# The second half of six matches moved from VectorE to ScalarE in a recommendation tower's opening

## What is computed

```
e = stack([tbl_k[ids[:, k]] for k in range(26)], axis=1)
combined = concatenate([dense[:, None, :], e], axis=1)
interactions = einsum('bnd,bmd->bnm', combined, combined)[:, TRIU_I, TRIU_J]
h = concatenate([dense, interactions, dense], axis=1)
h = maximum(h @ W_top1 + b_top1, 0)
h = maximum(h @ W_top2 + b_top2, 0)
y = h @ W_top3
```

## Time and profile before

| | before |
|---|---|
| median of 3 runs | 385.69 us |
| the profiled execution | 386.84 us |
| its span | 384.9 us |
| TensorE matmul busy | 343.2 us (89%) |
| VectorE busy | 193.3 us (50%) |
| ScalarE busy | 125.5 us (33%) |
| GpSimd busy | 251.9 us (65%) |
| mean granted TensorE clock | 0.986 |
| chain that ended last | PE 69%, POOL 17%, issue 8%, DVE 3% |

### The profile page before, as it was taken

How to read it: one execution, slowest core, us unless ns; L and a number is a source line. 1 busy time by engine, 2 the same in 40 slices (tenths; PEclk the granted TensorE clock), 3 DMA queues, 4 the chain that set the end, 5 groups by cost and what they waited for, 6 DMA issues and landing times.

```text
span 384.9 us, 13108 instructions
## 1 busy us (share of the span) xinstructions
PE 343.2 (89%) x6048; PEld 304.9 (79%) x6048; DVE 193.3 (50%) x94; ACT 125.5 (33%) x211; POOL 251.9 (65%) x267
## 2 busy tenths in 40 slices
PE   0787877889999999999999999999999999965995
PEld 0787767788888988889888988989888988854763
DVE  2799997577424872269243962288334942000000
ACT  2344432343233423343223423343223423322122
POOL 5777887777777777777777777777777777100200
PEclk9999999999999999999999999999999999968999
DMA  8996698253624362264525362256325332321300
GB/s 166 251 219 179 171 296 252 58 192 94 188 57 161 108 203 56 56 200 120 154 58 192 82 198 58 80 181 163 101 56 192 85 86 58 135 55 53 126 11 0
DMA packets 30869, 49.57 MB, mean 129 GB/s; under 512 B 17500, under 2 KB 17636, under 8 KB 30687
## 3 DMA queue, kind: packets, MB, share of 16 engines
q1 hardware_dynamic: 22494, 31.82, 27.7%
q0 software_dynamic: 8320, 16.92, 17.0%
HBM read 38.21 MB, written 10.49 MB: 127 GB/s over the span
## 4 chain that ended last, share of the span: by engine, by line
PE 69%; POOL 17%; issue 8%; DVE 3%; DMA 1%; ACT 1%; DVEq 0%
PE look_ps L309 26%; POOL rows L290 17%; PE mid_ps L339 12%; PE layer_ps L356 11%; PE layer_ps L365 7%; PE mid_ps L321 7%; PE layer_ps L353 4%; DVE match L450 3%; PE layer_ps L372 2%; DMA rows<-in_table,index 1%; DMA index<-in_index 1%; ACT hidden L515 0%; ACT hidden L521 0%; ACT turned L495 0%; ACT y_row L528 0%
## 5 line engine op out<-in xcount | busy, mean ns | idle before, releaser
L290 POOL DMA_INDIRECT rows<-in_table,index x256 | 248.7, 971 | 79.3 <-issue 77.7
L450 DVE TENSOR_TENSOR match<-look_ids,row_number_ps 125x2048 fp32r<-125x2048 int32 x80 | 181.8, 2287 | 126.0 <-PE look_ps L309 119.4
L309 PE MATMUL look_ps<-match,table_high 125*128 125x256 f32 x640 | 164.1, 294 | 21.3 <-DVE table_low L458 19.1
L309 PE MATMUL look_ps<-match,table_low 125*128 125x256 f32 x640 | 157.8, 284 | 0.3 <-issue 0.3
L309 PEld LDWEIGHTS look_ps<-match,table_high 125*128 125x128 f32 x640 | 123.3, 193 | 26.8 <-issue 16.8
L309 PEld LDWEIGHTS look_ps<-match,table_low 125*128 125x128 f32 x640 | 123.6, 193 | 0.0
L339 PEld LDWEIGHTS mid_ps<-turned 128*32 128x32 f32 x4096 | 45.6, 110 | 26.6 <-issue 22.7
L339 PE MATMUL mid_ps<-turned 128*32 128x27 f32 x4096 | 54.8, 196 | 12.5 <-issue 7.4
L488 ACT COPY turned<-look_ps 128x512 f32<-128x512 f32 x40 | 31.8, 799 | 68.3 <-PE look_ps L309 68.3
L495 ACT COPY turned<-mid_ps 128x512 f32<-128x512 f32 x64 | 42.9, 671 | 21.9 <-PE mid_ps L321 17.7
L356 PE MATMUL layer_ps<-pairs,w_pairs_sb 117*128 117x256 f32 x192 | 48.0, 386 | 0.0
(11 more groups left out here) (21 smaller groups left out, 44.8 us busy)
## 6 DMA issues: line engine op xcount, KB each, us to landing
look_ids<-in_look_rows SPq DMA_DIRECT2D x40, 256.0 KB
scratch<-grams SPq DMA_DIRECT2D x8, 864.0 KB
rows<-in_table,index POOLq DMA_INDIRECT x256
scratch<-grams SPq DMA_DIRECT2D x8, 416.0 KB
pairs<-scratch SPq DMA_DIRECT2D x92, 29.2 KB
grams<-in_table SPq DMA_DIRECT2D x4, 448.0 KB
pairs<-in_table SPq DMA_DIRECT2D x3, 448.0 KB
hidden<-in_table SPq DMA_DIRECT2D x3, 448.0 KB
```

The costliest lines, as they stand in the source:

```text
L290: pool.indirect_dma_start(out=rows[j % 2][:, at, :], out_offset=None, in_=tables[GATHERED[at]], in_offset=bass.IndirectOffsetOnAxis(ap=ind ...
L309: last = nc.tensor.matmul(look_ps[pair % 2][:, r % 2, :], part[0:table_rows, r, c, :], match[number % 2][0:table_rows, c, :], start=(c == ...
L450: nc.vector.tensor_tensor(match[number % 2][0:table_rows], look_ids[b][0:table_rows, r % 2].unsqueeze(1).broadcast_to(shape), row_number_p ...
```

## The change

For the first six looks of group 1, VectorE compares only parts 0 to 3. ScalarE makes parts 4 to 7 with two kinds of instruction: |id + (−row)| by Abs with the negated row number as a per-partition bias, one instruction for each of the four parts (256 elements), then Relu(1 − x) over all four (1024 elements), which is 1 where the id is the row and 0 elsewhere. Look (1, r) waits for both. VectorE makes the negated row numbers once. SyncE's loads of look ids into slots that these halves read wait for the halves too. On ScalarE the first half stands between split_high(0) and split_high(1), and the half for r = 1 to 5 at the head of the loop's round r, ahead of take_look and take_turned.

```diff
+        minus_row = sbuf("minus_row", [P, PARTS])
...
                 if number >= ID_SLOTS:
                     sp.wait_ge(match_ready, pair_end(number - ID_SLOTS))
+                    if ID_SLOTS <= number < ID_SLOTS + AHEAD:
+                        sp.wait_ge(second_halves, (number - ID_SLOTS + 1) // 2 * 2)
...
                 pe.wait_ge(match_ready, number + 1)
+                if g == 1 and r < AHEAD:
+                    pe.wait_ge(second_halves, r + 1)
...
-                shape = [table_rows, PARTS, N]
+
+                parts = PARTS // 2 if g == 1 and r < AHEAD else PARTS
+                shape = [table_rows, parts, N]
                 nc.vector.tensor_tensor(
-                    match[number % 2][0:table_rows],
+                    match[number % 2][0:table_rows, 0:parts],
                     look_ids[b][0:table_rows, r % 2].unsqueeze(1).broadcast_to(shape),
-                    row_number_ps[0:table_rows].unsqueeze(2).broadcast_to(shape),
+                    row_number_ps[0:table_rows, 0:parts].unsqueeze(2).broadcast_to(shape),
                     ALU.is_equal).then_inc(match_ready, 1)
...
+            nc.vector.tensor_scalar(minus_row[:], row_number[:], -1.0, None, ALU.mult).then_inc(row_numbers_copied, 1)
...
+            def match_second_half(r):
+
+                number, pair = look_number(1, r), pair_number(1, r // 2)
+                b = pair % ID_SLOTS
+                act.wait_ge(look_ids_in[b], 16 * (pair // ID_SLOTS + 1))
+                after(act, look_done, number - 1)
+                half = match[number % 2][0:table_rows, PARTS // 2:PARTS]
+                for c in range(PARTS // 2):
+                    last = nc.scalar.activation(half[:, c], look_ids[b][0:table_rows, r % 2], ACT.Abs,
+                                                bias=minus_row[0:table_rows, PARTS // 2 + c:PARTS // 2 + c + 1])
+                last.then_inc(distances_made, 1)
+                act.wait_ge(distances_made, r + 1)
+                flat = half.rearrange("p c n -> p (c n)")
+                nc.scalar.activation(flat, flat.bitcast(fp32), ACT.Relu, bias=1.0, scale=-1.0).then_inc(second_halves, 1)
...
-            for r in range(RAWS):
-                split_high(r)
+            split_high(0)
+            act.wait_ge(row_numbers_copied, 2)
+            match_second_half(0)
+            split_high(1)
+            split_high(2)
             for r in range(AHEAD):
+                if r > 0:
+                    match_second_half(r)
                 if r % 2 == 1:
                     take_look(0, r // 2)
                     take_look(1, r // 2)
```

More of the change, by code:

```diff
@@ L116, in build @@
         match_ready = sem("match_ready")
+        distances_made = sem("distances_made")
+        second_halves = sem("second_halves")
         look_done = sem("look_done")
@@ L463, in _ @@
             nc.vector.tensor_copy(row_number_ps[:], row_number[:]).then_inc(row_numbers_copied, 1)
+            nc.vector.tensor_scalar(minus_row[:], row_number[:], -1.0, None, ALU.mult).then_inc(row_numbers_copied, 1)
             for b in range(2):
                 nc.vector.memset(turned[b][:, N * FEATURES:], 0.0).then_inc(pads_zeroed, 1)
-            dve.wait_ge(row_numbers_copied, 1)
+            dve.wait_ge(row_numbers_copied, 2)
             for r in range(LOOKS):
```

## The result

The changed kernel took **396.59 us** (median of 4 runs, 393.57 to 398.02), the kernel before 385.76 in the same comparison (384.72 to 387.26): a ratio of 1.024, 95% interval 1.017 to 1.030. The forecast was 396.6 in a range of 391.7 to 402.5. Medians here are over all runs, while ratios leave out each run that lies over 1.5% above the fastest of its kernel, so the two can differ by some tenths of a percent.

The account below looks back on a forecast made before the run. Bound taken: GpSimd's gathers up to 88.48 us, then TensorE, with VectorE full in the opening. 386.84 + 9.0 − 1.8 + 3.7 = 397.7, less 1.15 for the median: 396.6 us, range 391.7 to 402.5.

Parts of the forecast that it names:

- ScalarE's order is the loss: Opening: each half waits behind the previous turn's copy and a cast, each look for its half; gram(0, 0) 9.0 us later.
- The total, 396.6: Whole kernel: forecast median 396.6 us, from 397.7 for the profiled execution less 1.15; chance of this case 0.50.
- the rival's sum: Opening: TensorE's clock cold in every round or halves nearer 3.1 us; 402.1 us, 1.8 more if both; chance 0.20.
- VectorE, 6.8 us less: Opening: six matches cut from 2048 to 1024 elements, about 1.1 us saved each, 6.8 us in all off VectorE.
- The half, 2.75 us: ScalarE's added work per look: four Abs 1.61, Relu 1.04, two hand-overs of 0.05; 2.75 us, between 2.5 and 3.1.
- Look(1, 1) at 26.06: Opening: its half waits for raw table 3 and a cast, so this look starts at 26.06 us instead of 20.93.
- Rounds of 6.89 and 7.10, look(1, 5) at 54.04: Opening loop: even rounds 6.89 us, odd 7.10, where a round was 5.7; the last of these looks starts at 54.04.
- The clock, 3.7 us: Opening: idle gaps drop TensorE's clock in the first round and one later one, 1.8 + 1.9 = 3.7 us more.
- Gather waits, −1.8: TensorE's two waits for gathered rows, 0.97 and 0.83 us, the second at turn(1, 7), vanish: 1.8 us back.
- In the opening VectorE is the full engine: Opening: VectorE's round is two matches, 4.70 us, and a split, 1.22; splits stand 5.7 us apart.
- The rival that was faster: Opening: splits miss GpSimd's gathers, so turn(1, 7) and the end come 3.1 us sooner, 382.6 us; chance 0.04.
- One that comes out early would stand at turn(1, 7): End of the gathers: a TensorE early out of the opening would still wait there for rows; the turn started at 91.10.

Follow-up runs that it names:

- the quarter: Against the changed kernel, ScalarE makes only parts 6 and 7 and VectorE six parts: 384.97 us, ratio 0.990; run once more 386.57 us, 1.001.

## Why the prediction was right

- *ScalarE's order is the loss*: right. With the same work in another place the ratio is 1.002 and not 1.015, and the waits for the halves are gone. Filler matmuls bring the ratio to 1.002 as well with the order as it is, so a large part of the loss is the cold clock behind the gaps that the order makes; the sum had both. The length of a step follows ScalarE's piece: with half of the match 7.0 and 7.2 us without a cold clock, with a quarter 5.8 and 6.0, 1.2 less for a piece that is 1.2 shorter.
- *The total, 396.6*: 396.59, and the closeness is luck. The sum made the profiled execution 397.7 and it took 396.51; taking off 1.15 for the median then hit, since the profile of the changed kernel lay at its own median. By its terms TensorE should have been 10.9 us late once the gathers' waits were used up, and it was 9.06; the growth behind that, which the sum did not have, made up for a part. On the second chip the loss was 5.7 us and not 10.8. The upper bound of 402.5 is not the rival's sum either, which is 402.1, or 403.9 with the slower halves.
- *VectorE, 6.8 us less*: 5.8. A match of 1024 elements took 1.22 us and not half of 2.28, so the matches are 6.4 us shorter in all.
- *The half, 2.75 us*: 2.93 from the first Abs to the look. The Abs took 1.71 for 1.61, the Relu 1.06 for 1.04, the wait on ScalarE's own result 0.02, the hand-over to TensorE 0.14 for 0.05. The self-wait, bounded at 0.3, cost nothing. The Trainium skill (ScalarE: Activation LUTs, What ACT_TABLE_LOAD costs) would have given the Abs from its rule, 280 ns + 0.833 a column with 93 ns of overlap, as 3 × 0.40 + 0.49 = 1.69 us, an estimate from that page, and the trace agrees with it better than with the row of layer 1. That row has another source (PSUM) and another input type; which of them makes it shorter no run shows. The surcharge for a pointer does not show in the Relu: 1.06 us at 1024 and 0.63 at 512 elements leave 0.20 as the fixed part. The same section of the Trainium skill gives 186 ns for the form with immediates, which agrees.
- *Look(1, 1) at 26.06*: 23.68. The step that was off is the landing of raw table 3, taken as 22.35: it came at 19.77, 8.95 us after its issue where it had taken 10.8. The wait itself was there; without it look(1, 1) started 2.3 us earlier.
- *Rounds of 6.89 and 7.10, look(1, 5) at 54.04*: 7.04 and 7.27 in the two uncold rounds, and 54.39. The closeness of the last number is luck: an earlier start (−2.4), slower rounds (+0.6) and the cold ones (+2.1), which the 54.04 did not include.
- *The clock, 3.7 us*: cold in the first round and one later one was the guess, 1.8 + 1.9. The first execution had 0.6 + 1.5 in these two rounds, some 0.3 in look(1, 5) and 1.3 behind gram(0, 0) (a place that was not foreseen), 3.7 in all. That cold rounds would come is confirmed, and the filler matmuls put their price at 4.3 us in another, colder execution; that the parts add up to the 3.7 of the forecast is luck.
- *Gather waits, −1.8*: the lateness fell from 11.13 to 10.00 at turn(1, 5) and from 10.04 to 9.06 at turn(1, 7), 2.1 us.
- *"In the opening VectorE is the full engine"*: true, and it misled about what relief could bring. The rival that was faster was argued away by ScalarE's loop and by GpSimd; what excludes it first is the buffer loop of 5.7 us, which was not seen. It did not change the forecast. The beat of the gathers, which this rival hoped to shorten by 3.1 us, moved little: in the kernels in which turn(1, 7) waits for its rows it starts at 89.65 to 91.88, where it started at 91.10.
- *"One that comes out early would stand at turn(1, 7)"*: right in kind, but the first floor is at turns (0, 6) and (0, 7), where an early opening has pulled the loads of the weights forward.

## What to carry to other kernels

Work given to an engine with idle time is only hidden where its inputs are ready before its neighbours in that engine's order: follow the loop look, copy, cast, half, look on paper before counting busy time. Before relieving a full engine, look for the second chain of the same length; here one match buffer per group made it, and a run with the relief for free showed it in one measurement. Idle stretches in TensorE can cost twice, once as the wait and once as a cold clock behind it, as in some of the rounds here, and filler matmuls are a cheap way to tell the two apart. Where two remedies give the same total, compare the starts of the same blocks in the profiles before saying that they mend the same thing.

## What was not expected of the hardware

- The clock fell after idle stretches of 1.6 us (before gram(0, 0)) and 1.8 us (before 31.50) and stayed up after 2.6 and 2.8 (before 40.08 and 47.35), in the same execution. In the profile of before it stayed up after 1.63 us ahead of gram(0, 0). The length of the gap alone does not decide.
- Seventy useless matmuls of 256 columns made the kernel 4.3 us faster.
- One kernel's runs scatter by up to 2.3% here (382.4 to 391.4 us for the kernel before on one chip), and a ratio from 6 runs of 0.990 (0.985 to 0.994) came out as 1.001 from 12. Between the copies of y for groups 5 and 6 pass 33.1 us in the profile of before and 29.7 in that of the quarter; before has stalls of up to 2.8 us inside Gram blocks there and a cold clock after them. The quarter's second profile has 29.4 with a ratio of 1.001, so this stretch alone does not explain the 0.990; what causes the stalls was not tested.
